# Looking up embeddings by one-hot matmuls and by gathers: nine features instead of seven in the first block, and one-hot work on both sides of the dot products

## Chip, core and metric
The kernel runs on one core of a Trainium2 chip. The metric is the device time of one execution in microseconds. TensorE (PE in the profile) multiplies, VectorE (DVE) and ScalarE (ACT) work element by element, GpSimd (POOL) issues the gathers here, and SyncE (SP) issues all other transfers. Each engine works through its own queue in order, and they meet at semaphores.

## What is computed
For each of 2048 samples, 27 rows of 128 numbers are looked up in 27 tables by the sample's ids. All 351 dot products between two different rows of a sample are taken, 16 dense numbers are appended, and three layers follow.

```
e = jnp.stack([tbl_0[ids[:, 0]], tbl_1[ids[:, 1]], ...], axis=1)
dot = jnp.einsum('bnd,bmd->bnm', inputs, inputs)
h = jnp.concatenate([z, dense_ctx], axis=1)
h = jnp.maximum(h @ W_top1 + b_top1, 0.0)
h = jnp.maximum(h @ W_top2 + b_top2, 0.0)
y = h @ W_top3
```

## The kernel before
The batch is cut into 8 blocks of 256 samples, a block into 2 tiles of 128. Two kinds of lookup exist.

**Gathered features.** 16 features (`GATHERED`) are fetched row by row: one indirect DMA on GpSimd's queue per feature and tile (line 353), into a ring of five buffers `rows` with four features each, a group. TensorE transposes a group into `tile_ps` (`tile_group`, line 605), ScalarE copies it into `samples` (`empty_group`, line 377). GpSimd may fill a ring buffer again when the group five before it has been transposed. Groups are counted through the kernel as n.

**One-hot features.** 11 features (`ONEHOT`) have tables of 1000 rows. Their tables are loaded once (line 238) through six staging buffers and split in a high half (`split_hi`, ScalarE, line 362) and a low half (`split_lo`, VectorE, line 501). For each block and feature SyncE loads the 256 ids, copied to all partitions (`idb`, line 229, a ring of three). VectorE compares them with row numbers (`masks`, line 494), and TensorE multiplies the masks with both halves (`onehot`, lines 593 and 595). A feature is four parts; a part is two masks and four matmuls. VectorE can be five parts ahead (`MASK_RING`), a block has 44 parts, counted from 0. Two features share a PSUM bank, a pair, which ScalarE copies out (`empty_onehot`, line 368).

**First block.** Its one-hots are made in a preamble, while tables still arrive. Only `NO_FIRST` = 7 features are looked up that way; the other four (`LATE`) are gathered for its two tiles, so these have five groups (20 gathers), all others four.

**Blocks.** Block b has 8 units. In each unit TensorE transposes the next tile's groups (`GROUPS_AT`), computes the dot products of 32 samples (`dot_unit`, line 621), and then does the unit's five or six parts for block b+1 (`unit_parts`, from `PARTS_UNTIL`). Layers of the block before follow: layer 3 in unit 0, the four steps of layer 1 in units 3 to 6, layer 2 in unit 7. `dot_unit` in units 0 and 4 waits until ScalarE has copied out all lookups of its samples. ScalarE copies dots out (`empty_dots`, line 396), and in block 0 splits w1 after unit 4's dots and w2 after unit 5's; VectorE makes their low halves after the masks of parts 28 and 33 (lines 509 and 516).

**SyncE's queue.** After a block SyncE issues, in this order: the ids of the third feature of the block after next (a load that waits until mask 43 is made), four stores of the dots to DRAM (line 269), one load of ids, the dense numbers, after the stores have landed the loads that bring the dots back with one product per partition (`load_z`, lines 278 and 280), and then the next ids. VectorE splits what came back in `z_hi` and `z_lo` (`split_z`, line 532) in unit 3, for layer 1. In the preamble the queue holds tables and ids by turns, then the weights (`load_weights`, lines 245 to 251), then the ids of block 1 from feature 3 on. The last block stores and reloads its dots in two halves.

## Time and profile before
| | |
|---|---|
| three runs | 379.4, 377.6, 384.47 us (median 379.4) |
| the profiled execution | 376.98 us, of which the span 375.2 us |
| mean granted clock of TensorE | 0.973 of full speed |
| TensorE busy | 331.5 us, 88% of the span |
| GpSimd busy | 252.3 us, 67%, in 264 gathers |
| VectorE busy | 250.1 us, 67% |
| ScalarE busy | 134.3 us, 36% |

Busy times of matmuls are modelled, and TensorE works on several at once. GpSimd's share leaves out the short pauses between gathers. An average over the span hides that the front (to about 100 us) and the tail (from about 342 us) have limits of their own, so the stretches are read one by one.

### The profile page before, as it was taken

The numbers are of one execution on the slowest core, as the hardware profiler recorded it, in microseconds if no ns is written. First come the engines' busy times: TensorE is split into PE (matmuls) and PEld (weight loads), VectorE is DVE, ScalarE is ACT, GpSimd is POOL, SyncE is SP. The second block draws the span as 40 slices with busy tenths as digits, with TensorE's granted clock in tenths as the row PEclk, the third lists the DMA queues.
The fourth block names the chain that finished last, engine by engine and source line by source line (L and its number), as shares of the span: only waits on it lengthen the run. The fifth ranks groups of instructions, "written<-read, shape, count | busy, mean of one in ns | idle before, by whom it ended". The sixth has DMA issues, their size and how long they took to land.

```text
span 375.2 us, 14179 instructions
## 1 busy us (share of the span) xinstructions
PE 331.5 (88%) x6216; PEld 302.7 (81%) x6216; DVE 250.1 (67%) x757; ACT 134.3 (36%) x235; POOL 252.3 (67%) x271
## 2 busy tenths in 40 slices
PE   0776679788799999999999999999899999996786
PEld 0665679678699988998999988998799988995775
DVE  3899577697477669765876769666776769622031
ACT  2353424532222533333333343333233343344122
POOL 5777777777777777777777777777777777760000
PEclk9999698999899999999999999999999999999699
DMA  7999954248644665348544754447634755354410
GB/s 171 239 214 231 225 142 100 81 94 190 115 91 96 141 146 113 84 90 193 127 80 101 162 131 105 93 107 178 112 87 94 163 125 113 79 120 90 79 41 1
DMA packets 59215, 46.39 MB, mean 124 GB/s; under 512 B 38499, under 2 KB 53186, under 8 KB 59153
## 3 DMA queue, kind: packets, MB, share of 16 engines
q1 hardware_dynamic: 50705, 28.16, 35.0%
q0 software_dynamic: 8448, 17.32, 19.6%
q8 instruction: 49, 0.80, 0.9%
q14 instruction: 13, 0.11, 0.1%
HBM read 38.37 MB, written 7.09 MB: 121 GB/s over the span
## 4 chain that ended last, share of the span: by engine, by line
PE 62%; DMA 12%; POOL 11%; DVE 8%; issue 6%; ACT 1%; POOLq 0%
PE onehot_ps L593 16%; PE onehot_ps L595 13%; POOL rows L353 11%; PE dots_ps L621 10%; DMA idb<-ids_onehot 8%; DVE mask L494 7%; PE tile_ps L605 6%; PE mlp_ps L627 5%; PE mlp_ps L629 5%; PE mlp_ps L628 5%; DMA rows<-tbl,idx 3%; PE mlp_ps L662 2%; DMA idx<-ids_gather 1%; DVE z_lo L532 0%; DVE z_hi L529 0%
## 5 line engine op out<-in xcount | busy, mean ns | idle before, releaser
L353 POOL DMA_INDIRECT rows<-tbl,idx x264 | 251.5, 953 | 82.5 <-issue 79.6
L494 DVE TENSOR_SCALAR mask<-idb,cmp 125x256 fp32r<-125x256 int32 x672 | 208.8, 381 | 54.1 <-PE onehot_ps L595 32.2
L593 PE MATMUL onehot_ps<-mask,tab_hi 125*128 125x256 f32 x672 | 175.9, 300 | 28.5 <-DVE mask L494 17.6
L595 PE MATMUL onehot_ps<-mask,tab_lo 125*128 125x256 f32 x672 | 166.3, 284 | 0.0
L593 PEld LDWEIGHTS onehot_ps<-mask,tab_hi 125*128 125x128 f32 x672 | 129.6, 193 | 35.7 <-DVE mask L494 17.1
L595 PEld LDWEIGHTS onehot_ps<-mask,tab_lo 125*128 125x128 f32 x672 | 130.3, 194 | 0.0
L621 PEld LDWEIGHTS dots_ps<-emb 128*27 128x27 f32 x4096 | 45.4, 106 | 19.6 <-issue 16.4
L377 ACT COPY emb<-tile_ps 128x512 f32<-128x512 f32 x66 | 44.1, 671 | 46.9 <-PE tile_ps L605 45.4
L621 PE MATMUL dots_ps<-emb 128*27 128x27 f32 x4096 | 54.8, 194 | 6.3 <-issue 5.6
L368 ACT COPY emb<-onehot_ps 128x512 f32<-128x512 f32 (+1 forms) x46 | 36.3, 789 | 57.3 <-PE onehot_ps L595 54.7
L605 PE MATMUL tile_ps<-ident,rows 128*128 128x128 f32 x264 | 40.9, 279 | 4.5 <-DMA rows<-tbl,idx 4.5
L539 DVE SCALAR_TENSOR_TENSOR h_lo<-mlp_ps,h_hi 128x512 fp32r<-128x512 f32 x16 | 11.1, 692 | 43.7 <-ACT h_hi L402 43.7
L605 PEld LDWEIGHTS tile_ps<-ident,rows 128*128 128x128 f32 x264 | 30.7, 143 | 7.8 <-issue 7.7
L396 ACT COPY dots<-dots_ps 128x216 f32<-128x216 f32 x64 | 21.7, 339 | 28.7 <-PE dots_ps L621 28.5
L627 PE MATMUL mlp_ps<-z_hi,w_hi 125*128 125x256 f32 (+1 forms) x96 | 28.2, 294 | 0.5 <-ACT h L421 0.5
L628 PE MATMUL mlp_ps<-z_hi,w_lo 125*128 125x256 f32 (+1 forms) x96 | 27.9, 290 | 0.0
L629 PE MATMUL mlp_ps<-z_lo,w_hi 125*128 125x256 f32 (+1 forms) x96 | 27.9, 290 | 0.0
L402 ACT ACTIVATE h_hi<-mlp_ps 128x512 fp32r<-128x512 f32 x16 | 9.6, 597 | 47.2 <-PE mlp_ps L629 47.2
L362 ACT CAST tab_hi<-emb 125x1024 fp32r<-125x1024 f32 x11 | 11.5, 1047 | 25.6 <-DMA emb<-tbl 25.6
L627 PEld LDWEIGHTS mlp_ps<-z_hi,w_hi 125*128 125x128 f32 (+1 forms) x96 | 19.1, 199 | 1.0 <-ACT h L421 1.0
L627 PE MATMUL mlp_ps<-h_hi,w_hi 128*128 128x256 f32 x64 | 18.2, 284 | 1.4 <-DVE h_lo L539 1.4
L628 PEld LDWEIGHTS mlp_ps<-z_hi,w_lo 125*128 125x128 f32 (+1 forms) x96 | 19.1, 199 | 0.0
(30 smaller groups left out, 153.0 us busy)
## 6 DMA issues: line engine op xcount, KB each, us to landing
idb<-ids_onehot SPq DMA_DIRECT2D x84, 128.0 KB
dots_dram<-dots SPq DMA_DIRECT2D x28, 216.0 KB
emb<-tbl SPq DMA_DIRECT2D x11, 448.0 KB
rows<-tbl,idx POOLq DMA_INDIRECT x264
zT<-dots_dram SPq DMA_DIRECT2D x14, 117.0 KB
dots_dram<-dots SPq DMA_DIRECT2D x8, 108.0 KB, 2.9
zT<-dots_dram SPq DMA_DIRECT2D x7, 104.0 KB
emb<-tbl SPq DMA_DIRECT2D x11, 52.0 KB
```

Of the source, the lines that this page charges most:

```text
L353: nc.gpsimd.indirect_dma_start(rows[:, n % RING, i, :], None, tables[feature][:, :], bass.IndirectOffsetOnAxis(idx[:, at:at + 1], 0)).then ...
L368: nc.scalar.copy(samples[b % 2][:, :, NG + a:NG + z], onehot_ps[:, pair(b, v) % 2, 0:(z - a) * BLK].rearrange("p (k b) -> p b k", k=z - a) ...
L377: nc.scalar.copy(samples[b % 2][:, q * P:(q + 1) * P, at:at + GROUP], tile_ps[:, n % 2, :].rearrange("p (k b) -> p b k", k=GROUP)).then_in ...
L396: nc.scalar.copy(dst[:, :, at:at + UNIT_Q], dots_ps[:, u % 2, 0:UNIT_Q * FEATURES].rearrange("p (c j) -> p j c", c=UNIT_Q)).then_inc(dots_ ...
L494: made = nc.vector.tensor_scalar(mask[0:VP, n % MASK_RING, c, :], idb[0:VP, k % IDB_RING, :], cmp[0:VP, at:at + 1], None, ALU.is_equal)
L593: nc.tensor.matmul(out, tab_hi[0:VP, f, at, :], mask[0:VP, k % MASK_RING, c, :], start=(at == 0), stop=False)
L595: done = nc.tensor.matmul(out, tab_lo[0:VP, f, at, :], mask[0:VP, k % MASK_RING, c, :], start=False, stop=(at == CHUNKS - 1))
L605: done = nc.tensor.transpose(tile_ps[:, n % 2, i * P:(i + 1) * P], rows[:, n % RING, i, :], ident[:, :])
L621: done = nc.tensor.matmul(dots_ps[PAD * s:PAD * s + FEATURES, u % 2, i * FEATURES:(i + 1) * FEATURES], sample, sample, start=True, stop=True)
L627: nc.tensor.matmul(out, w_hi, x_hi, start=first, stop=False)
L628: nc.tensor.matmul(out, w_lo, x_hi, start=False, stop=False)
L629: return nc.tensor.matmul(out, w_hi, x_lo, start=False, stop=last)
```

## The change
Nine features instead of seven are looked up by one-hot in the first block. The last group of its two tiles then has two gathers instead of four (`group_size`), 18 a tile; the index arrays and the counts of the `gathered` semaphores follow (`GROUP_AT`, `RING_USES`). Its transposes stand after other features (`FIRST_GROUPS_AT`). In each unit two parts now stand between the transposes and the dots, two between the dots and the layers, and the rest behind the layers, on TensorE and in ScalarE's copies. In the last block SyncE puts the dense numbers behind the first half's stores and loads that half back ahead of the second half's stores. VectorE's code is unchanged; its lookups follow `NO_FIRST`.

```
-NO_FIRST = 7
+NO_FIRST = 9
-NGR_FIRST = NGR + len(LATE) // GROUP
+NGR_FIRST = NGR + 1
+def group_size(g):
+    return GROUP if g < NGR else len(LATE)
+GROUP_LIST = [(t, g) for t in range(NT) for g in range(groups(t))]
+GROUP_AT = [sum(group_size(g) for _, g in GROUP_LIST[:n]) for n in range(len(GROUP_LIST) + 1)]
+BEFORE_DOTS, BEFORE_LAYERS = 2, 4
-FIRST_GROUPS_AT = {1: 0, 2: 1, 3: 2, 5: 3, 6: 4}
+FIRST_GROUPS_AT = {1: 0, 2: 1, 4: 2, 5: 3, 6: 4}
+def pair_ends(f, h):
+    return h == PARTS - 1 and (f % 2 == 1 or f == NO - 1)
...
# SyncE
+            for f in range(NO - NO_FIRST, IDB_RING):
+                load_idb(1, f)
             load_weights()
...
                 store_dots(LAST, q * P * half, dots[:, LAST % 2, q * half:(q + 1) * half], NQ // TILES,
                            last_out[q])
-            load_dense(LAST)
-            for q in range(TILES):
+                if q == 0:
+                    load_dense(LAST)
                 sp.wait_ge(last_out[q], 16 * QUAD)
...
# GpSimd
-                    for i in range(GROUP):
+                    for i in range(group_size(g)):
...
# ScalarE
+                    parts = unit_parts(u) if b < LAST else []
+                    for f, h in parts[:BEFORE_DOTS]:
+                        if pair_ends(f, h):
+                            empty_onehot(b + 1, f // 2)
                     empty_dots(b, u)
+                    for f, h in parts[BEFORE_DOTS:BEFORE_LAYERS]:
+                        if pair_ends(f, h):
+                            empty_onehot(b + 1, f // 2)
...
+                    for f, h in parts[BEFORE_LAYERS:]:
+                        if pair_ends(f, h):
+                            empty_onehot(b + 1, f // 2)
...
# TensorE
+                    for f, h in parts[:BEFORE_DOTS]:
+                        onehot(b + 1, f, h)
                     dot_unit(b, u)
-                    if b < LAST:
-                        for f, h in unit_parts(u):
-                            onehot(b + 1, f, h)
+                    for f, h in parts[BEFORE_DOTS:BEFORE_LAYERS]:
+                        onehot(b + 1, f, h)
                     if b > 1 and u == LAYER3_AT:
                         layer3(b - 2)
...
+                    for f, h in parts[BEFORE_LAYERS:]:
+                        onehot(b + 1, f, h)
```

TensorE, block 0, the start of unit 4. Before:

```order
L605 MATMUL tile_ps<-ident,rows 128x128 [waits gathered0,tile_ps_empty]
L605 MATMUL tile_ps<-ident,rows 128x128 x3
L621 MATMUL dots_ps<-emb 27x27 [waits onehot_ps_empty,tile_ps_empty,dots_ps_empty]
L621 MATMUL dots_ps<-emb 27x27 x31
L593 MATMUL onehot_ps<-mask,tab_hi 128x256 [waits mask_ready]
L595 MATMUL onehot_ps<-mask,tab_lo 128x256
```

The same place in the changed kernel:

```order
L631 MATMUL tile_ps<-ident,rows 128x128 [waits gathered0,tile_ps_empty]
L631 MATMUL tile_ps<-ident,rows 128x128 x3
L619 MATMUL onehot_ps<-mask,tab_hi 128x256 [waits mask_ready,onehot_ps_empty]
L621 MATMUL onehot_ps<-mask,tab_lo 128x256
L619 MATMUL onehot_ps<-mask,tab_hi 128x256
L621 MATMUL onehot_ps<-mask,tab_lo 128x256
L619 MATMUL onehot_ps<-mask,tab_hi 128x256 [waits mask_ready]
L621 MATMUL onehot_ps<-mask,tab_lo 128x256
L619 MATMUL onehot_ps<-mask,tab_hi 128x256
L621 MATMUL onehot_ps<-mask,tab_lo 128x256
L647 MATMUL dots_ps<-emb 27x27 [waits onehot_ps_empty,tile_ps_empty,dots_ps_empty]
L647 MATMUL dots_ps<-emb 27x27 x31
```

Eight one-hot matmuls, two parts, have moved ahead of the unit's 32 dot products (line 621 before is line 647 now).

SyncE, the end of the preamble's queue, from the last id load ahead of the weights on. Before:

```order
L229 DMA idb<-ids_onehot 128x256 [waits mask_ready]
L238 DMA emb<-tbl 112x1024 [waits lo_ready]
L238 DMA emb<-tbl 13x1024
L245 DMA dots<-w 125x512 x2
L245 DMA dots<-w 117x512
L247 DMA dots<-b 1x512
```

In the changed kernel:

```order
L246 DMA idb<-ids_onehot 128x256 [waits mask_ready]
L255 DMA emb<-tbl 112x1024 [waits lo_ready]
L255 DMA emb<-tbl 13x1024
L246 DMA idb<-ids_onehot 128x256 [waits mask_ready] x2
L262 DMA dots<-w 125x512 x2
L262 DMA dots<-w 117x512
L264 DMA dots<-b 1x512
```

Two id loads, each waiting for masks, now stand between the last table and the weights.

ScalarE, block 0, units 6 and 7 (lines 377, 396 and 368 copy a transposed group, dots, and a one-hot pair). Before:

```order
L377 COPY emb<-tile_ps 128x128x4 [waits tile_ps_full]
L396 COPY dots<-dots_ps 128x27x8 [waits dots_ps_full]
L377 COPY emb<-tile_ps 128x128x4 [waits tile_ps_full]
L396 COPY dots<-dots_ps 128x27x8 [waits dots_ps_full]
L368 COPY emb<-onehot_ps 128x256x2 [waits mask_used]
L368 COPY emb<-onehot_ps 128x256 [waits mask_used]
```

In the changed kernel:

```order
L400 COPY emb<-tile_ps 128x128x4 [waits tile_ps_full]
L419 COPY dots<-dots_ps 128x27x8 [waits dots_ps_full]
L400 COPY emb<-tile_ps 128x128x4 [waits tile_ps_full]
L390 COPY emb<-onehot_ps 128x256x2 [waits mask_used]
L419 COPY dots<-dots_ps 128x27x8 [waits dots_ps_full]
L390 COPY emb<-onehot_ps 128x256 [waits mask_used]
```

The copy of the pair that ends with part 39 now stands ahead of the copy of unit 7's dots.

## Rows read from the trace of the kernel before

**Rows 1.** Page, costly groups: line, engine, operation, count | busy us, mean ns | idle before

```profile
L353 POOL DMA_INDIRECT rows<-tbl,idx x264 | 251.5, 953 | 82.5 <-issue 79.6
```

**Rows 2.** Timeline of GpSimd: start us, us, engine, line, operation [idle before, releaser]

```profile
334.62 0.95 POOL L353 DMA_INDIRECT rows<-tbl,idx  x1 [0.31 <-issue]
```

**Rows 3.** Time windows: window, busy us per engine, granted clock, DMA share, GB/s

```profile
core 0: us, PE busy (x) PEld busy (x) DVE busy (x) ACT busy (x) POOL busy (x), PEclk, DMA share, GB/s
40.00:88.50 48.50, 41.41 (x817) 37.94 (x818) 36.10 (x109) 18.39 (x34) 36.64 (x39) 0.91 0.58 134
...
56.00:58.00 2.00, 2.00 (x11) 2.00 (x11) 2.00 (x8) 0.71 (x1) 1.64 (x2) 0.50 0.39 87
...
131.00:173.00 42.00, 41.50 (x788) 38.19 (x787) 30.17 (x99) 15.09 (x27) 31.86 (x34) 1.00 0.55 122
...
135.11:137.92 2.81, 2.81 (x24) 2.81 (x25) 2.13 (x8) 1.16 (x2) 2.20 (x3) 1.00 0.60 178
```

**Rows 4.** Timeline of TensorE, transposes at unit 7, unit 4 and unit 7

```profile
121.68 0.60 PE L605 MATMUL tile_ps<-ident,rows 128*128 128x128 f32 x4
...
148.45 0.60 PE L605 MATMUL tile_ps<-ident,rows 128*128 128x128 f32 x4
...
163.05 0.60 PE L605 MATMUL tile_ps<-ident,rows 128*128 128x128 f32 x4
```

**Rows 5.** Timeline of TensorE, block 0

```profile
40.56 1.09 PE L605 MATMUL tile_ps<-ident,rows 128*128 128x128 f32 x4 [3.43 <-DMA rows<-tbl,idx]
...
54.12 0.38 PE L593 MATMUL onehot_ps<-mask,tab_hi 125*128 125x256 f32 x1 [2.04 <-DVE mask L494]
...
63.31 0.60 PE L605 MATMUL tile_ps<-ident,rows 128*128 128x128 f32 x4
...
69.67 0.39 PE L593 MATMUL onehot_ps<-mask,tab_hi 125*128 125x256 f32 x1 [1.45 <-DVE mask L494]
```

**Rows 6.** Timeline of VectorE, preamble to block 1

```profile
30.30 1.26 DVE L501 TENSOR_TENSOR tab_lo<-emb,tab_hi 125x1024 fp32r<-125x1024 f32 x1
...
34.04 1.27 DVE L501 TENSOR_TENSOR tab_lo<-emb,tab_hi 125x1024 fp32r<-125x1024 f32 x1
35.23 3.16 DVE L494 TENSOR_SCALAR mask<-idb,cmp 125x256 fp32r<-125x256 int32 x10
...
53.45 6.63 DVE L494 TENSOR_SCALAR mask<-idb,cmp 125x256 fp32r<-125x256 int32 x22 [2.69 <-DMA idb<-ids_onehot]
...
67.13 1.90 DVE L509 TENSOR_TENSOR w_lo<-dots,w_hi 125x512 fp32r<-125x512 f32 x3 [2.32 <-ACT w_hi L426]
...
75.54 9.31 DVE L494 TENSOR_SCALAR mask<-idb,cmp 125x256 fp32r<-125x256 int32 x30
...
98.62 2.48 DVE L494 TENSOR_SCALAR mask<-idb,cmp 125x256 fp32r<-125x256 int32 x8 [4.75 <-DMA idb<-ids_onehot]
```

**Rows 7.** Timeline of SyncE's queue, preamble, and the stores after blocks 0 and 1

```profile
37.24 1.08 SPq L245 DMA_DIRECT2D dots<-w  x3
...
43.31 18.84 SPq L229 DMA_DIRECT2D idb<-ids_onehot  x6
...
82.03 4.05 SPq L269 DMA_DIRECT2D dots_dram<-dots  x4
...
125.31 4.22 SPq L269 DMA_DIRECT2D dots_dram<-dots  x4
```

**Rows 8.** Timeline of ScalarE, the copy of the pair that ends with part 31

```profile
71.70 0.79 ACT L368 COPY emb<-onehot_ps 128x512 f32<-128x512 f32 x1 [2.85 <-PE onehot_ps L595]
```

**Rows 9.** Timeline of VectorE, block 2

```profile
140.60 2.51 DVE L494 TENSOR_SCALAR mask<-idb,cmp 125x256 fp32r<-125x256 int32 x8 [1.76 <-DMA idb<-ids_onehot]
...
146.98 0.42 DVE L532 TENSOR_TENSOR z_lo<-zT,z_hi 118x256 fp32r<-118x256 f32 x1
```

**Rows 10.** Timeline of TensorE, layer 1 of the last block

```profile
363.21 0.39 PE L627 MATMUL mlp_ps<-z_hi,w_hi 125*128 125x256 f32 x1 [0.45 <-ACT h L421]
```

More of the change, by code:

```diff
@@ L84, in group_slot @@
     return GROUP * g if g < NGR else NG + NO_FIRST
+def group_size(g):
+    return GROUP if g < NGR else len(LATE)
+GROUP_LIST = [(t, g) for t in range(NT) for g in range(groups(t))]
+GROUP_AT = [sum(group_size(g) for _, g in GROUP_LIST[:n]) for n in range(len(GROUP_LIST) + 1)]
+RING_USES = [sum(group_size(GROUP_LIST[k][1]) for k in range(n % RING, n + 1, RING)) for n in range(len(GROUP_LIST))]
 UNIT_Q = 8
@@ L142, in build @@
         rows = sb("rows", [P, RING, GROUP, D], f32)
-        idx = sb("idx", [P, group(NT, 0) * GROUP], i32)
+        idx = sb("idx", [P, GROUP_AT[-1]], i32)
         idb = sb("idb", [P, IDB_RING, BLK], i32)
@@ L350, in _ @@
                         pool.wait_ge(tile_ps_full, n - RING + 1)
-                    for i in range(GROUP):
-                        feature, at = SLOTS[group_slot(g) + i], GROUP * n + i
+                    for i in range(group_size(g)):
+                        feature, at = SLOTS[group_slot(g) + i], GROUP_AT[n] + i
                         nc.gpsimd.indirect_dma_start(
@@ L365, in empty_onehot @@
             def empty_onehot(b, v):
+                if b == 1 and v == 0:
+                    act.wait_ge(lo_ready, NO)
                 a, z = 2 * v, min(2 * v + 2, looked_up(b))
@@ L376, in empty_group @@
                 act.wait_ge(tile_ps_full, n + 1)
-                nc.scalar.copy(samples[b % 2][:, q * P:(q + 1) * P, at:at + GROUP],
-                               tile_ps[:, n % 2, :].rearrange("p (k b) -> p b k", k=GROUP)
+                k = group_size(g)
+                nc.scalar.copy(samples[b % 2][:, q * P:(q + 1) * P, at:at + k],
+                               tile_ps[:, n % 2, 0:k * P].rearrange("p (k b) -> p b k", k=k)
                                ).then_inc(tile_ps_empty, 1)
@@ L602, in tile_group @@
                     pe.wait_ge(tile_ps_empty, n - 1)
-                pe.wait_ge(gathered[n % RING], 16 * GROUP * (n // RING + 1))
-                for i in range(GROUP):
+                pe.wait_ge(gathered[n % RING], 16 * RING_USES[n])
+                for i in range(group_size(g)):
                     done = nc.tensor.transpose(tile_ps[:, n % 2, i * P:(i + 1) * P], rows[:, n % RING, i, :],
@@ L677, in _ @@
                     t = TILES * b + u // UNITS_TILE + 1
+                    parts = unit_parts(u) if b < LAST else []
                     for g in GROUPS_AT[u % UNITS_TILE]:
@@ L680, in _ @@
                             tile_group(t, g)
+                    for f, h in parts[:BEFORE_DOTS]:
+                        onehot(b + 1, f, h)
                     dot_unit(b, u)
-                    if b < LAST:
-                        for f, h in unit_parts(u):
-                            onehot(b + 1, f, h)
+                    for f, h in parts[BEFORE_DOTS:BEFORE_LAYERS]:
+                        onehot(b + 1, f, h)
                     if b > 1 and u == LAYER3_AT:
@@ L734 @@
         "ids_gather": _np.stack([ids[t * P:(t + 1) * P, SLOTS[group_slot(g) + i]] for t in range(NT)
-                                 for g in range(groups(t)) for i in range(GROUP)], axis=1),
+                                 for g in range(groups(t)) for i in range(group_size(g))], axis=1),
         "ids_onehot": ids[:, ONEHOT].T,
```

4 lines of the change are left out of this document (removed).

## Prediction

> **What bounds the kernel now.** I read the page's table of costly groups first, then the time windows, then the timelines of each engine in the first two blocks and in one later block.
>
> GpSimd issues 264 gathers of 0.95 us with 0.30 us between them [rows 1]. The last starts at 334.62 us [rows 2]: 264 x 1.256 = 331.6 us, so it runs almost from start to end of that stretch without a wait. It looks like the pace setter and is not: from the second block on it is several groups ahead. TensorE in block 2 is busy 41.50 of 42 us [rows 3]; a later block is bound by TensorE. From unit 7 to unit 7 a block takes 163.05 - 121.68 = 41.37 us [rows 4].
>
> Block 0 is different. TensorE is busy only 41.41 of 48.5 us, part of it at half clock: the granted clock in 56 to 58 us is 0.50 [rows 3], 1.2 of 2.4 GHz, after 2.04 us of idling [rows 5]. Its waits are for gathered rows (3.43 us at 40.56) and for masks (2.04 at 54.12, 1.45 at 69.67) [rows 5]. VectorE in turn waits there for a feature's ids (2.69) and for ScalarE's half of the w1 split (2.32) [rows 6]. So the front of the kernel hangs on VectorE, its inputs and SyncE's queue, the rest on TensorE.
>
> **Prices.** A part (4 matmuls of 256 columns) costs TensorE 2.81 / 6 = 0.47 us [rows 3]. VectorE makes 30 masks in 9.31 us [rows 6], 0.62 us a part. From the tile transposes at 63.31 to part 29 at 69.67 [rows 5] lie two transposes-plus-dots, five parts and the wait: (6.36 - 1.45 - 2.35) / 2 = 1.28 us for one group's transposes with one unit of dots, of which I give 0.75 to the dots.
>
> **Four gathers fewer.** They take 4 x 1.256 = 5.0 us off GpSimd. Between 0 and -5.0 us; I take 0, because the gathers for block 2 on are finished before they are wanted. The 3.43 us wait at 40.56 goes too, but the next item covers it.
>
> **Two more features in the preamble.** 16 masks, 2 table splits (moved forward), 32 matmuls. The splits of consecutive features start 34.04 - 30.30 = 3.74 us apart [rows 6], and that is VectorE's pace per feature, TensorE's matmuls hiding behind it. Before, the last mask of the preamble is done at about 35.9 (the first pair of the ten from 35.23 [rows 6]); now 35.9 + 7.5 = 43.4. The 12 parts of block 1 that follow, with the one split left, need 12 x 0.62 + 1.2 = 8.6 us: VectorE wants the ids of feature 3 at 52.0.
>
> **SyncE's queue.** It now issues two more id loads before the weights, and the last of these waits for all 36 preamble parts (43.4). The weights therefore start at 43.9 instead of 37.24, and since they take 43.31 - 37.24 = 6.1 us to issue [rows 7], the ids of feature 3 are issued at 50.0 instead of 43.31. Before, they landed at 53.45 [rows 6], 10.1 us after issue, queued behind weights and a table. The price now is not in the trace. The table is older by then, the weights are not. Floor: landed before they are wanted, 52.0. Ceiling: again 10.1 us, 60.1. I take 54.7, nearer the floor: the same bytes as before plus two id loads (0.25 MB at the 134 GB/s of this stretch [rows 3] is 1.9 us at most, and I take 1.3) after the old 53.4. TensorE resumes at 55.4, 1.3 us later than at 54.12.
> The Trainium skill (DMA: Bandwidth & Descriptors, Latency and other measured facts) speaks of about 2 us of fixed cost per DMA. By it alone the load would be in at about 52 and VectorE would not wait; the old load's 10.1 us speaks against using it with a full queue.
>
> **Interleaving in block 0.** From part 12 to unit 4's transposes it took 63.31 - 54.12 = 9.19 us [rows 5]; one unit of dots more and two transposes less give 9.85: unit 4 starts at 65.25 (+1.9). The w1 split in ScalarE's queue sits behind the dots of unit 4, VectorE's half behind it [rows 6], and masks from part 29 on behind that. Two parts now stand ahead of these dots: 0.94 us more. Part 29 starts at 65.25 + 6.36 + 0.94 = 72.55 (+2.9). The w2 split comes after ScalarE's copy of the pair that ends with part 31, which was at 71.70 [rows 8]; a unit of dots now stands between parts 30 and 31: 0.7 us more. Part 34's mask starts at 72.55 + (75.54 - 69.67) + 0.7 = 79.1 against 75.54, part 43's is made 6.2 us later, at 85.3, and SyncE, which waits for it with an id load ahead of the stores, starts storing at 85.6 against 82.03 [rows 7]: **+3.6 us**. Bounds: 0 if the ids are never late, +6 if the 3.1 us idling that this puts before parts 29 and 34 drops the clock as 2.04 us did.
>
> **Block 1** follows the stores: from there to the mask of part 16, which had waited 4.75 us for its ids, 98.62 - 82.03 = 16.6 us [rows 6, 7]. Same chain, +3.6 us stays.
>
> **Blocks 2 to 6.** Take L, the end of layer 1's fourth step, as zero (121.68 [rows 4]). Then the stores start at 3.6 (125.31 [rows 7]), released by mask 43 and not by the dots; mask 16 starts at 18.9 and z_lo's third part is done at 25.7 [rows 9]; unit 4 starts at 26.8 (148.45) and the next L comes 14.6 later [rows 4]. The new order moves the dots of unit 7 to L + 2.9, still done with their copy when mask 43 is. So the DMA chain stays. On TensorE one part less lies before layer 1's first step (part 38 went behind L, parts 22 and 23 behind the step): it waits for z_lo until 25.7, ends at 26.1, parts 22 and 23 put unit 4 at 27.0 (+0.2), and the rest is 14.1 (-0.5). 41.1 instead of 41.37. Bounds -0.6 and +1.2 a block; I take -0.2, five times: **-1.1**. The ends of the chain: -0.5 in block 1 (part 38), +0.4 before block 7 (part 43 behind layer 2).
>
> **The last block.** The dense load goes ahead of the second half's stores, and z of the first half is loaded ahead of them. TensorE's start on the last block's layer 1 at 363.21 waits for ScalarE (0.45 us), not for z [rows 10]. 0.
>
> **Sum:** 3.6 - 0.5 - 1.1 + 0.4 = +2.4 us on the profiled execution's 376.98 us (span 375.2), 379.4. That execution is 2.4 us under the 379.4 us median of the runs, and the fastest run is 377.6; I state the forecast between these two scales, **380.0 us**.
>
> **Rivals.**
> - *The gathers are the pace after all.* Then 5.0 us come through and with them the 3.43 us wait: 376.98 - 8.4 = 368.5. For it: 331.6 us without a gap [rows 1, 2]. Against: TensorE at 41.50 of 42 [rows 3]. 0.10.
> - *The ids of feature 3 land in time* (below 52.0). Then VectorE never stops, the clock stays up, and unit 4 starts at 61.5 to 62.7: 2.6 to 3.8 us off the sum, 375.6 to 376.8, a small gain. 0.15.
> - *The loop gets longer (the other side).* The dots of unit 7 now come 1.4 us later after L, and ScalarE copies a one-hot pair (0.79 us [rows 8]) ahead of theirs. If that copy ends more than about 0.3 us after mask 43, the stores move, and with them everything to z_lo: 0.7 to 1.2 us in each of six blocks, 4 to 7 us: 383.6 to 386.6. The idling before parts 29 and 34 adds up to 2.4 at half clock: up to 389. 0.20.
> - *Nothing adds:* within 376.8 to 383, the forecast. 0.50. The remaining 0.05 lies above 389.
>
> **How the numbers follow.** The range takes in the second rival, the forecast and most of the third: 373 to 388. A change of 2% is 7.6 us, about what a measurement of this kernel can tell from none. Faster by over 2%: the first rival and a little, 0.12. Slower: most of the third and the rest, 0.20. Within: 0.68.
>
> **What would show it.** In the changed profile: preamble one-hots end near 44 with no wait for gathered rows after them; the first mask wait in block 0 near part 12 at 54 to 55; waits of about 3 us before parts 29 and 34; first stores at 85 to 86; block period 41.1 with a wait for z_lo before layer 1; GpSimd waiting for transposes for the first time. The forecast is wrong if the first stores come before 82, or if the period is below 40.5 or above 42.

## The result: slower, with the loss in the front

| | before | after |
|---|---|---|
| four runs each, same chip | 377.6 to 384.47 us, median 380.23 | 385.76 to 387.23 us, median 386.95 |
| ratio (95% interval) | | 1.024 (1.020 to 1.028) |
| span of the profiled execution | 375.2 us | 385.2 us |
| mean granted clock of TensorE | 0.973 | 0.969 |

The changed kernel is 6.7 us slower by the medians, 2.4%. The time lies inside the forecast range (373 to 388), 7 us above the forecast itself. I called a change within 2% likeliest; the kernel is slower beyond its interval, by about 2% or a little more. In a second measurement the changed kernel had 387.09 us against 379.32 (1.016, 0.996 to 1.037). Here and below a median takes all executions, a ratio leaves out those over 1.5% above the fastest of their kernel, so the two need not agree. The profiled execution of before is 3.3 us under the median of its runs, so the spans differ by more than the medians, 10.0 us; the steps below are followed on that scale.

The page of the changed kernel, TensorE's two rows of slices, the group that answers to [rows 1], and TensorE's one-hots:

```profile
PE   0867859779869999999999999999999998997777
PEclk9999997969969999999999999999999999999899
...
L372 POOL DMA_INDIRECT rows<-tbl,idx x260 | 249.5, 960 | 90.0 <-issue 74.8
L619 PE MATMUL onehot_ps<-mask,tab_hi 125*128 125x256 f32 x688 | 190.7, 309 | 33.6 <-DVE mask L520 23.0
```

Four gathers fewer bring nothing here: GpSimd now idles instead, as its pauses for transposes show (13.0 us in 14 of them). The granted clock falls in slices 7, 9 and 12, which begin at 58, 77 and 106 us. TensorE waited 23.0 us for masks in all.

**The front.** TensorE, at the places of [rows 5] and at the start of block 1:

```profile
58.16 0.58 PE L619 MATMUL onehot_ps<-mask,tab_hi 125*128 125x256 f32 x1 [5.09 <-DVE mask L520]
...
68.31 0.60 PE L631 MATMUL tile_ps<-ident,rows 128*128 128x128 f32 x4
...
75.42 0.38 PE L619 MATMUL onehot_ps<-mask,tab_hi 125*128 125x256 f32 x1 [2.77 <-DVE mask L520]
...
83.36 0.39 PE L619 MATMUL onehot_ps<-mask,tab_hi 125*128 125x256 f32 x1 [2.48 <-DVE mask L520]
...
91.92 0.60 PE L631 MATMUL tile_ps<-ident,rows 128*128 128x128 f32 x4
...
109.08 0.55 PE L619 MATMUL onehot_ps<-mask,tab_hi 125*128 125x256 f32 x1 [4.82 <-DVE mask L520]
```

Part 12 comes 4.0 us later than before, unit 4's transposes 5.0, part 29 5.75. Part 34 comes 7.15 later (before it stood at 76.21 after a wait of 1.96), block 1 8.8 (before at 83.11). The three waits ahead of parts 12, 29 and 34 are 5.09, 2.77 and 2.48 us, where 2.04, 1.45 and 1.96 had stood.

VectorE, at the places of [rows 6]:

```profile
46.34 5.01 DVE L520 TENSOR_SCALAR mask<-idb,cmp 125x256 fp32r<-125x256 int32 x16
57.46 2.63 DVE L520 TENSOR_SCALAR mask<-idb,cmp 125x256 fp32r<-125x256 int32 x8 [6.10 <-DMA idb<-ids_onehot]
...
72.88 1.89 DVE L535 TENSOR_TENSOR w_lo<-dots,w_hi 125x512 fp32r<-125x512 f32 x3 [3.44 <-ACT w_hi L449]
...
80.84 1.10 DVE L542 TENSOR_TENSOR w_lo<-zT,w_hi 128x256 fp32r<-128x256 f32 x3 [3.12 <-ACT w_hi L455]
...
82.68 1.55 DVE L520 TENSOR_SCALAR mask<-idb,cmp 125x256 fp32r<-125x256 int32 x5
```

It stands idle 6.10 us for the ids of feature 3, then 3.44 and 3.12 us for ScalarE's halves of the splits. SyncE's queue, the answer to [rows 7]:

```profile
43.20 2.12 SPq L262 DMA_DIRECT2D dots<-w  x3
...
49.48 2.23 SPq L246 DMA_DIRECT2D idb<-ids_onehot  x3
...
90.89 4.27 SPq L286 DMA_DIRECT2D dots_dram<-dots  x4
```

The weights are issued from 43.20 instead of 37.24, the ids of feature 3 at 49.48 instead of 43.31, and they are in at 57.46. The first stores start at 90.89, 8.9 us later.

What releases these stores is new. The mask for part 43 is made at 89.23 (end of the six masks from 87.33), but the stores start 0.02 us after ScalarE's copy of unit 7's dots, which is done at 90.87:

```profile
87.33 1.90 DVE L520 TENSOR_SCALAR mask<-idb,cmp 125x256 fp32r<-125x256 int32 x6 [0.35 <-PE onehot_ps L621]
...
90.53 0.34 ACT L419 COPY dots<-dots_ps 128x216 f32<-128x216 f32 x1 [0.46 <-PE dots_ps L647]
```

Before, that copy was done at 81.13, ahead of mask 43 (about 81.7, an estimate from the pace of the 30 masks in [rows 6]), and the stores followed the mask.

**Windows** of the changed kernel, the answer to [rows 3] (busy us per engine, granted clock, DMA share, GB/s):

```profile
42.00:44.00 2.00, 1.16 (x10) 1.16 (x11) 2.00 (x8) 1.43 (x2) 1.49 (x2) 1.00 0.50 86
44.00:46.00 2.00, 2.00 (x76) 1.83 (x75) 2.00 (x6) 1.08 (x3) 1.39 (x3) 1.00 0.33 48
46.00:48.00 2.00, 1.82 (x13) 1.48 (x13) 2.00 (x7) 0.08 (x1) 1.70 (x2) 1.00 0.55 194
...
58.00:60.00 2.00, 1.84 (x8) 1.78 (x8) 2.00 (x7) 0.00 (x0) 1.41 (x2) 0.50 0.26 66
...
78.00:80.00 2.00, 2.00 (x11) 2.00 (x11) 0.00 (x0) 1.18 (x4) 1.70 (x2) 0.50 0.59 109
...
84.00:86.00 2.00, 2.00 (x68) 1.77 (x69) 2.00 (x8) 0.00 (x0) 1.39 (x3) 0.50 0.51 78
```

And two of these windows in the kernel before:

```profile
42.00:44.00 2.00, 2.00 (x55) 1.94 (x45) 0.26 (x1) 0.00 (x0) 1.70 (x2) 0.50 1.09 212
44.00:46.00 2.00, 2.00 (x15) 2.00 (x15) 1.83 (x7) 1.35 (x2) 1.39 (x3) 0.78 1.13 246
```

From 42 to 46 us the transfers move 86 and 48 GB/s where they had moved 212 and 246: the weights, the next large transfers in the queue, stand behind an id load that waits for masks. They are issued from 43.20 on, but it is 46 us before the rate is up again (194). After each of the three waits in block 0 there are windows at half clock (0.50, 1.2 GHz).

**Blocks 2 to 6.** TensorE's transposes at unit 7 of block 1 and of block 6, and layer 1's wait for z_lo in block 2:

```profile
131.91 0.60 PE L631 MATMUL tile_ps<-ident,rows 128*128 128x128 f32 x4
...
157.23 0.39 PE L653 MATMUL mlp_ps<-z_hi,w_hi 118*128 118x256 f32 x1 [0.51 <-DVE z_lo L558]
...
339.83 0.60 PE L631 MATMUL tile_ps<-ident,rows 128*128 128x128 f32 x4
```

Before, the last of these stood here:

```profile
330.20 0.60 PE L605 MATMUL tile_ps<-ident,rows 128*128 128x128 f32 x4
```

The period, the average length of these blocks, is (339.83 - 131.91) / 5 = 41.58 us; before, (330.20 - 121.68) / 5 = 41.70 us over the same five blocks, with 121.68 from [rows 4]. These blocks are as long as they were: the loss is there by 132 us. The average before holds one long block (246.04 to 288.92, 42.88 us); its other four took 41.28 to 41.59 us, the five of the changed kernel 41.38 to 41.91. A last 0.6 us is added behind block 7's first transposes (346.32, where 336.91 stood, +9.4).

### The profile page after: what moved, and what is told of

It is laid out like the page before. It is cut to its first block, busy times and chain, and to the rows that moved or that the text cites. A ratio compares the mean times of both kernels' runs of the same rounds, so it can differ in the third digit from the quotient of the medians.

```text
span 385.2 us, 14253 instructions
## 1 busy us (share of the span) xinstructions
PE 336.6 (87%) x6244; PEld 309.6 (80%) x6244; DVE 256.1 (66%) x773; ACT 134.5 (35%) x236; POOL 250.3 (65%) x267
## 4 chain that ended last, share of the span: by engine, by line
PE 50%; DVE 17%; DMA 16%; SPq 11%; issue 3%; ACT 3%; DVEq 0%
PE onehot_ps L619 14%; PE onehot_ps L621 12%; DVE mask L520 11%; PE dots_ps L647 8%; DMA dots_dram<-dots 7%; DMA idb<-ids_onehot 6%; PE tile_ps L631 4%; SPq L295 4%; SPq L286 4%; PE mlp_ps L653 4%; PE mlp_ps L655 3%; PE mlp_ps L654 3%; DVE tab_lo L527 3%; DMA emb<-tbl 2%; DVE z_lo L558 1%
## 5 line engine op out<-in xcount | busy, mean ns | idle before, releaser
L520 DVE TENSOR_SCALAR mask<-idb,cmp 125x256 fp32r<-125x256 int32 x688 | 214.7, 381 | 50.6 <-DMA idb<-ids_onehot 25.5
L619 PE MATMUL onehot_ps<-mask,tab_hi 125*128 125x256 f32 x688 | 190.7, 309 | 33.6 <-DVE mask L520 23.0
L621 PE MATMUL onehot_ps<-mask,tab_lo 125*128 125x256 f32 x688 | 176.1, 287 | 0.0
L619 PEld LDWEIGHTS onehot_ps<-mask,tab_hi 125*128 125x128 f32 x688 | 134.6, 196 | 42.6 <-DVE mask L520 23.0
L621 PEld LDWEIGHTS onehot_ps<-mask,tab_lo 125*128 125x128 f32 x688 | 135.3, 197 | 0.2 <-issue 0.2
L400 ACT COPY emb<-tile_ps 128x512 f32<-128x512 f32 (+1 forms) x66 | 44.7, 678 | 50.0 <-PE tile_ps L631 49.9
L419 ACT COPY dots<-dots_ps 128x216 f32<-128x216 f32 x64 | 21.7, 339 | 81.3 <-PE dots_ps L647 73.9
L390 ACT COPY emb<-onehot_ps 128x512 f32<-128x512 f32 (+1 forms) x47 | 37.2, 791 | 35.1 <-PE onehot_ps L621 35.1
L631 PE MATMUL tile_ps<-ident,rows 128*128 128x128 f32 x260 | 39.7, 275 | 0.0
L655 PEld LDWEIGHTS mlp_ps<-z_lo,w_hi 125*128 125x128 f32 (+1 forms) x96 | 18.8, 196 | 0.0
```

Of the source, the lines that this page charges most:

```text
L390: nc.scalar.copy(samples[b % 2][:, :, NG + a:NG + z], onehot_ps[:, pair(b, v) % 2, 0:(z - a) * BLK].rearrange("p (k b) -> p b k", k=z - a) ...
L400: nc.scalar.copy(samples[b % 2][:, q * P:(q + 1) * P, at:at + k], tile_ps[:, n % 2, 0:k * P].rearrange("p (k b) -> p b k", k=k)).then_inc( ...
L419: nc.scalar.copy(dst[:, :, at:at + UNIT_Q], dots_ps[:, u % 2, 0:UNIT_Q * FEATURES].rearrange("p (c j) -> p j c", c=UNIT_Q)).then_inc(dots_ ...
L520: made = nc.vector.tensor_scalar(mask[0:VP, n % MASK_RING, c, :], idb[0:VP, k % IDB_RING, :], cmp[0:VP, at:at + 1], None, ALU.is_equal)
L619: nc.tensor.matmul(out, tab_hi[0:VP, f, at, :], mask[0:VP, k % MASK_RING, c, :], start=(at == 0), stop=False)
L621: done = nc.tensor.matmul(out, tab_lo[0:VP, f, at, :], mask[0:VP, k % MASK_RING, c, :], start=False, stop=(at == CHUNKS - 1))
```

## Experiments

Each ratio is to the kernel before, measured alongside on the same chip, with its 95% interval. Times in the text are of the profiled execution, from the start of its span. "Unit 4" is block 0's.

### One part of the change alone

Nine features, with the old order and the old last block:

```
-BEFORE_DOTS, BEFORE_LAYERS = 2, 4
+BEFORE_DOTS, BEFORE_LAYERS = 0, 8
 # SyncE, last block: load_dense(LAST) and all loads of z behind both halves' stores again
```

> Nine features in the first block with everything else as before (parts all behind the unit's dots, last block's loads as before). Theory 1 (the front: two more features push the weights behind two id loads that wait for masks, the ids of feature 3 land at about 57 and TensorE takes up part 12 at about 58 instead of 54.12): 382 to 385 us, about 5 to 7 us over before, of which 4 us are there at part 12 and the rest comes from clock and block 1. Waits before parts 29 and 34 as before, 1.5 and 2 us. Rival 2 (the new order is what costs, the nine features are nearly free): at most 380 us.

Measured: median 381.76 us, ratio 1.005 (1.001 to 1.009), span 377.2. It came below the 382 to 385 us that I expected.

```profile
68.27 0.60 PE L631 MATMUL tile_ps<-ident,rows 128*128 128x128 f32 x4
...
74.65 0.39 PE L619 MATMUL onehot_ps<-mask,tab_hi 125*128 125x256 f32 x1 [1.45 <-DVE mask L520]
```

Unit 4 is as late as in the changed kernel (68.27 and 68.31): the delay up to there comes from the two features. The waits ahead of parts 29 and 34 are the old ones (1.45, and 1.02). The stores start at 87.04, +5.0 us. Blocks 2 to 6, at 41.41 us each, give back 1.5 us of it, and the span ends at +2.0.

The new order with seven features, and the old last block:

```
-NO_FIRST = 9
+NO_FIRST = 7
-FIRST_GROUPS_AT = {1: 0, 2: 1, 4: 2, 5: 3, 6: 4}
+FIRST_GROUPS_AT = {1: 0, 2: 1, 3: 2, 5: 3, 6: 4}
```

> The new order alone: seven features, parts on both sides of the dots, last block's loads as before. Theory 1: the ids of feature 3 land at 53.4 as before; only the waits before parts 29 and 34 grow (from 1.45 and 1.96 to about 2.8 and 2.5 us, with half clock behind them): 379 to 381.5 us, 2 to 4 us over before; block period 41.3 to 41.6 us. Rival 2: 384 us and more.

Measured: median 382.24 us, ratio 1.008 (1.003 to 1.012), span 380.9.

```profile
76.66 0.39 PE L619 MATMUL onehot_ps<-mask,tab_hi 125*128 125x256 f32 x1 [3.23 <-DVE mask L520]
...
121.92 0.60 PE L631 MATMUL tile_ps<-ident,rows 128*128 128x128 f32 x4
...
190.74 0.39 PE L653 MATMUL mlp_ps<-z_hi,w_hi 118*128 118x256 f32 x1 [0.98 <-DVE z_lo L558]
...
335.07 0.60 PE L631 MATMUL tile_ps<-ident,rows 128*128 128x128 f32 x4
```

The order alone lengthens the waits ahead of parts 29 (2.12 us at 69.29) and 34 (3.23), though the clock stays up here and the stores start only 1.2 us late (83.24). What it loses it loses later: (335.07 - 121.92) / 5 = 42.63 us a block, with a wait of about 1 us for z_lo in each. The changed kernel has the same code in these blocks and takes 41.58. I had expected 41.3 to 41.6, and 379 to 381.5 us in all; that difference gets two runs below.

With the clock up, this run also tells what the order costs at the end of block 0. The mask of part 34 starts at 75.94 and the stores at 83.24, again 0.02 us after the dots' copy:

```profile
82.88 0.34 ACT L419 COPY dots<-dots_ps 128x216 f32<-128x216 f32 x1 [0.65 <-PE dots_ps L647]
```

That is 7.30 us, where it takes 6.49 us in the kernel before and 6.48 with nine features in the old order.

The changed kernel with the last block as before:

```
-                if q == 0:
-                    load_dense(LAST)
+            load_dense(LAST)
+            for q in range(TILES):
                 sp.wait_ge(last_out[q], 16 * QUAD)
```

> The changed kernel with only the last block's stores and loads put back to the order of before. Theory: the three short waits of the last layer 1 for z_lo (0.99, 0.28 and 0.31 us) go and ScalarE's 0.45 us comes back: 0.3 to 0.8 us less than the changed kernel. Rival: the tail's 0.7 us is scatter of the dots' stores, no difference beyond 0.3 us.

Measured: median 384.73 us, ratio 1.015 (1.008 to 1.022), span 382.5. From block 7's first transposes (344.48) to the end it takes 38.0 us; the changed kernel 385.2 - 346.32 = 38.9. TensorE, last layer 1, changed kernel:

```profile
372.57 0.35 PE L653 MATMUL mlp_ps<-z_hi,w_hi 125*128 125x256 f32 x1 [0.99 <-DVE z_lo L558]
```

Two more waits for z_lo follow, of 0.28 and 0.31 us. With the old last block the same place has the 0.45 us wait for ScalarE of [rows 10] again, and none for z_lo. So with the first half loaded back ahead, layer 1 waits for what comes last. The price is not shown: that stretch takes 38.0 to 39.7 us in the three profiles with the new order and the old last block, and 38.4 to 40.7 us in the eight with the new one, and the measured times do not separate it either. On this chip the parts add up: by the medians the two features cost 2.2 us, the order 2.7, both together (this run) 5.2.

### Mending one suspected cost

The weights behind block 1's first ids:

```
-            load_weights()
             for b in range(BLOCKS):
...
                 if b < LAST:
                     load_idb(b + 1, IDB_RING)
+                if b == 0:
+                    load_w1()
...
                     for f in range(IDB_RING + 2, NO):
                         load_idb(b + 1, f)
+                        # b == 0: w2 and w3 follow the ids of the sixth and the seventh feature
```

> The changed kernel with SyncE's weights issued behind the ids of block 1: w1 and b1 behind feature 3's ids, w2 behind feature 5's, w3 and b2 behind feature 6's. Theory 1: VectorE's 6.10 us wait for ids shrinks to 1 us or less, part 12 starts at 53 to 54 instead of 58.16, no half clock there, unit 4 of block 0 at 62 to 63 instead of 68.31; 380.5 to 383 us. Rival 3 (the DMA engines are short there in any order, the wait only moves to a later id load): part 12 early, but another id wait of 3 us or more behind it, 385 us or more.

Measured: median 384.43 us, ratio 1.012 (1.004 to 1.021), span 379.1.

```profile
58.01 0.36 PE L627 MATMUL onehot_ps<-mask,tab_hi 125*128 125x256 f32 x1 [1.59 <-DVE mask L528]
...
63.44 0.60 PE L639 MATMUL tile_ps<-ident,rows 128*128 128x128 f32 x4
```

The wait of 5.09 us at part 12 is gone. The one of 1.59 us is a new one, four parts later: VectorE waits 2.80 us (to 57.18) for the ids of feature 4, which now stand behind w1. So the late load was in part only moved, as the rival had it, but by less than the 3 us named there. Unit 4 starts at 63.44, where it had started before the change, 4.9 us earlier than in the changed kernel, and the stores start at 86.07 (90.89): the weights ahead of the ids cost 4.9 us there. The profile, of the fastest of the four executions (380.86), shows it more plainly than the times, whose median came above what I expected (380.5 to 383).

Then the changed kernel once more, on the chip of the next three:

> The changed kernel once more, as the yardstick of the three below on one chip: 1.5 to 2.5% over before, id wait of 5 to 6 us in block 0, waits before parts 29 and 34 of 2.5 to 3 us.

Measured: median 387.09 us (382.37 to 390.74) against 379.32 (ratio above). The profiled execution (388.53) waits at the same places, ahead of parts 12, 29 and 34: 5.34, 2.93 and 3.37 us. Its period is 42.04 us, where the first profile had 41.58.

ScalarE's halves of the w1 and w2 splits one unit earlier:

```
-                    if b == 0 and u == 4:
+                    if b == 0 and u == 3:
                         split_w1_hi()
-                    if b == 0 and u == 5:
+                    if b == 0 and u == 4:
                         split_w2_hi()
```

> The changed kernel with ScalarE's halves of the w1 and w2 splits one unit earlier in its queue, behind units 3 and 4 of block 0 instead of 4 and 5. Theory (VectorE waits for ScalarE, who waits for a unit's dots that now come two parts later): VectorE's waits of 3.44 and 3.12 us go, TensorE's 2.77 and 2.48 us before parts 29 and 34 shrink below 0.5 us each and the half clock there with them, block 1 starts 4 to 6 us earlier, the whole is 4 to 6 us shorter than the changed kernel. Rival (VectorE is simply behind with its masks): the waits move to parts 30 to 38, less than 2 us shorter.

Measured: median 379.9 us, ratio 1.008 (1.003 to 1.014), span 379.3. The median is 7.2 us under the changed kernel's on the same chip; by the ratios (1.008 against 1.016, the latter with a wide interval) it is some 3 us, and by the spans of the two profiles (379.3 and 385.2) 5.9.

```profile
84.48 0.60 PE L631 MATMUL tile_ps<-ident,rows 128*128 128x128 f32 x4
```

One wait of 0.58 us is left of the two, the clock stays up from 64 to 100 us, and block 1 starts at 84.48 instead of 91.92, 7.4 us earlier. The part-12 wait is untouched (4.82). So the splits that stand behind the dots in ScalarE's queue are the larger of the two costs.

Both together:

> The changed kernel with both of the two mends of its front: the weights behind block 1's first ids, and ScalarE's halves of the w1 and w2 splits one unit earlier. My theory: what the change loses in the front is the late weights queue (4.9 us up to unit 4 of block 0, in the run with the weights moved) and the two mask waits behind the splits with their half clock (some 6 us, in the run with the splits moved), and the two are at different places, so they add up: block 1 starts at 79.5 to 81 us instead of 91.9, and the time falls to 374 to 377 us, below the kernel before. Rival: the second is only hidden idling of the same DMA or mask chain, so that the two together give what one gave: 379 to 381 us. In both the block period stays at 41.6 us.

Measured: median 376.84 us, ratio 0.996 (0.991 to 1.001), span 374.9.

```profile
58.42 0.35 PE L627 MATMUL onehot_ps<-mask,tab_hi 125*128 125x256 f32 x1 [2.02 <-DVE mask L528]
...
81.37 0.60 PE L639 MATMUL tile_ps<-ident,rows 128*128 128x128 f32 x4
```

Block 1 starts at 81.37, 10.5 us earlier than in the changed kernel: more than either alone (4.8 and 7.4), less than their sum. The wait at 58.42, part 16's, is followed by half clock here, and unit 4 starts at 65.45 instead of 63.44. With both mended the front's loss is gone, and the kernel is level with the one before. The period was 41.83 us, where I had expected 41.6.

### What sets the length of blocks 2 to 6

By the prediction's step on these blocks it is the chain stores, loads of z, ids, masks, z_lo. If so, an id load that stands behind the loads of z, and with them behind the wait for the stores, is what to move. In the kernel before:

```
                 if b > 0:
                     load_dense(b - 1)
+                if b < LAST:
+                    load_idb(b + 1, IDB_RING + 1)
+                if b > 0:
                     sp.wait_ge(dots_out[(b - 1) % 2], 16 * QUAD * ((b - 1) // 2 + 1))
                     load_z(b - 1, 0, slice(0, BLK), NQ, z_in)
-                if b < LAST:
-                    load_idb(b + 1, IDB_RING + 1)
```

> The kernel before, with one load of ids (feature 4 of the next block) moved ahead of the wait for the stores and the loads of z in SyncE's queue. Theory (in the old order the chain stores, z loads, ids, masks, z_lo is just short of being the limit, except in blocks 1 and 5): VectorE's wait for ids before part 16 goes (4.75 us in block 1), TensorE's 2.64 us there too; the period of blocks 2 to 6 falls from 41.7 to 40.8 to 41.2 us; 4 to 7 us under before. Rival (TensorE's work is the period): only block 1 gains, 2 to 3 us.

Measured: median 373.56 us, ratio 0.989 (0.977 to 1.002), span 371.7. Unit 7 of block 1, of block 6, and a transpose of the last tile:

```profile
121.72 0.60 PE L606 MATMUL tile_ps<-ident,rows 128*128 128x128 f32 x4
...
323.76 0.60 PE L606 MATMUL tile_ps<-ident,rows 128*128 128x128 f32 x4
...
338.84 0.41 PE L606 MATMUL tile_ps<-ident,rows 128*128 128x128 f32 x2 [3.31 <-DMA rows<-tbl,idx]
```

The period is 40.41 us, 1.3 less, and of VectorE's waits for ids in blocks 2 to 6 one of 0.15 us is left. TensorE has the same work in these blocks, so its work was not what set their length before. The interval of the ratio still reaches 1. Now GpSimd is late at the end: TensorE waits 3.31 us for rows that did not hold it up before.

The same move in the changed kernel:

> The changed kernel with the same move of one id load. Theory (in the new order that chain is the period): the waits for z_lo before layer 1 (0.5 to 0.9 us a block) go, the period falls from 41.6 to 40.8 to 41.1 us, TensorE's 4.82 us wait in block 1 shrinks below 1.5 us: 6 to 9 us under the changed kernel. Rival (the z loads are what is late, not the masks queued ahead of the z splits): the waits for z_lo stay, at most 4 us, all from block 1.

Measured: median 377.52 us, ratio 0.998 (0.993 to 1.002), span 375.5. The median is 9.6 us under the changed kernel's on the same chip, the span 9.7 us under the 385.2 of its first profile. The period is (330.36 - 127.14) / 5 = 40.64 us, the waits for z_lo are gone there, and block 1's wait at part 16 falls from 4.82 to 0.94. The three waits of block 0 stay (4.75, 2.46, 2.94).

### All of it: what order and features are worth then

The changed kernel with all three mends:

> The same with the id load of a block's fifth feature ahead of the loads that bring the dots back. It took the block period from 41.6 to 40.7 us in the changed kernel. If that holds here too, 4.6 us come off: 369.5 to 372.5 us. Rival: GpSimd now limits (its 260 gathers of 1.256 us cannot have the last one started before 329.6 us), shown by waits for gathered rows in the last two blocks: 373 us or more.

Measured: median 368.63 us, ratio 0.975 (0.970 to 0.981), span 367.3, period 40.84. That is a little under what I expected. There is no wait for rows in the last two blocks, but GpSimd never pauses for more than 0.31 us, and its last gather starts at 330.84.

The same with the old order in every unit:

> The same again, but with a unit's parts all behind its dots, as in the kernel before, in every unit (nine features in the first block, the new last block). If the interleaved order costs something by itself wherever VectorE's masks are short, this one is faster by up to 2 us: 368.5 to 371 us, with a period of 40.4. Rival: with the waits gone the order is worth something, and this one is slower than the interleaved kernel of this call by over 1 us.

Measured: median 367.63 us, ratio 0.975 (0.969 to 0.981), span 366.2, period 40.51. The two cannot be told apart by time (367.16 to 369.51 and 367.17 to 369.9). That does not show that the order is worth nothing. With the old order TensorE comes to block 7 3.8 us earlier (324.29 against 328.08) and then waits 1.87 and 2.18 us for rows, so that its last transposes start at 333.65, against this in the new order:

```profile
334.32 0.66 PE L640 MATMUL tile_ps<-ident,rows 128*128 128x128 f32 x4
```

In both the last gather starts at 330.8 us. The gathers hide what the old order gains; what it would be worth without them is not measured.

The kernel before with the same three mends:

> The kernel before (seven features, its own order, 264 gathers) with the same three mends. It tells what the two features more are worth once nothing else is in the way. GpSimd's last gather cannot start before 334.6 us here, against 329.6 with 260 gathers. If GpSimd limits by now, it waits for rows in block 0 and in the last two blocks and takes 2 to 4 us more than the nine-feature kernel in the same order: 372 to 374 us. Rival: the preamble, 7.5 us shorter on VectorE, gives more than the gathers cost: 367 to 370 us, below the nine-feature kernel.

Measured: median 372.58 us, ratio 0.988 (0.982 to 0.993), span 370.6, period 40.67. Two of its rows, TensorE's last wait for gathered rows and GpSimd's last gather (in block 0 it also waits 2.97 and 2.57 us for rows):

```profile
338.74 1.09 PE L614 MATMUL tile_ps<-ident,rows 128*128 128x128 f32 x4 [3.26 <-DMA rows<-tbl,idx]
...
335.56 0.94 POOL L362 DMA_INDIRECT rows<-tbl,idx  x1 [0.30 <-issue]
```

With nine features, old order:

```profile
333.65 1.09 PE L640 MATMUL tile_ps<-ident,rows 128*128 128x128 f32 x4 [2.18 <-DMA rows<-tbl,idx]
...
330.85 1.09 POOL L381 DMA_INDIRECT rows<-tbl,idx  x1 [0.30 <-issue]
```

Now the last gather is what the end waits for. It starts 4.7 us earlier with nine features, and TensorE's last transposes 5.1 us earlier. That is close to the 5.0 us between the medians, and to the 4 x 1.256 us of the prediction's step on the gathers. The two kernels differ in the last block too, which is 0.7 us longer in the nine-feature one from there to the end. What was worth nothing in the change is worth some 5 us here: the kernel had to be limited by GpSimd first.

### Why 42.63 and 41.58 us with the same code

GpSimd paused for about 2 us beside stores and loads of z in the changed kernel, and never with seven features. To force the pause with seven, four ring buffers instead of five:

```
-RING = 5
+RING = 4
```

> Seven features in the new order, with a ring of four instead of five buffers for gathered rows. With five, its blocks 2 to 6 took 42.64 us each though the changed kernel, with the same code there, took 41.58. My theory: GpSimd's gathers share the DMA engines with the loads that bring the dots back. In the changed kernel GpSimd is ahead and pauses for about 2 us, for a ring buffer, just while stores and loads are under way; with seven features it never pauses, and the chain from the first store to z_lo's third part takes 22.4 to 23.0 us instead of 21.6. With four buffers it must pause there too: the chain falls to 21.6 to 21.8 and the period to 41.5 to 41.9. The total may rise, since block 0 has less in store. Rival: the 1 us comes from where the features' masks lie or from the place of the instructions, and period and chain stay at 42.4 or more.

Measured: median 383.75 us, ratio 1.010 (1.005 to 1.015), span 380.7, period 42.06. From the stores to z_lo's third part it took 22.7, 22.2, 21.9, 21.9 and 22.1 us in blocks 2 to 6, with pauses of about 2 us in all in the last two alone. The period lies between what the two theories gave. The chain is shorter than with five buffers (22.4 to 23.0), but no shorter where the pauses are: block 4, without one, has the same 21.9 as block 5 with one.

The changed kernel with the last two features of the first tiles gathered twice (the index arrays and the semaphore counts follow):

```
-                    for i in range(group_size(g)):
-                        feature, at = SLOTS[group_slot(g) + i], GROUP_AT[n] + i
+                    for i in range(GROUP):
+                        feature, at = SLOTS[group_slot(g) + i % group_size(g)], GROUP_AT[n] + i
```

> The changed kernel, but each of the first block's two tiles gathers its last two features twice, so that GpSimd issues 264 gathers as before (the second copies are not used). It prices the four gathers fewer by themselves. By my prediction they are worth 0. By the theory of the pauses GpSimd gets ahead 5 us later, so that in some blocks it does not pause beside the loads: up to 1 us a block, 387 to 391 us, with a chain of 22.4 us or more in each block where no pause of GpSimd falls in the first 9 us after the stores start. Rival: nothing hangs on them, 385.5 to 387.5 us, with the period at 41.6.

Measured: median 387.12 us, ratio 1.014 (1.002 to 1.025), span 385.8, period 41.83. The changed kernel had 386.95 and 387.09 in its two measurements. These times could not tell 4 us from nothing, but the profile agrees with 0, as predicted: TensorE waits for rows only once, 0.84 us in the preamble, and GpSimd still pauses, 6.9 us in all. Block 3 of this run, stores and z_lo's third part, with no pause of GpSimd in between:

```profile
176.08 3.98 SPq L286 DMA_DIRECT2D dots_dram<-dots  x4
...
197.47 0.42 DVE L558 TENSOR_TENSOR z_lo<-zT,z_hi 118x256 fp32r<-118x256 f32 x1
```

That is 21.4 us. Block 5, with a pause:

```profile
259.12 2.50 SPq L286 DMA_DIRECT2D dots_dram<-dots  x3
...
263.11 0.95 POOL L372 DMA_INDIRECT rows<-tbl,idx  x1 [1.02 <-PE tile_ps L631]
...
281.71 0.43 DVE L558 TENSOR_TENSOR z_lo<-zT,z_hi 118x256 fp32r<-118x256 f32 x1
```

That is 22.6 us, longer with the pause than without. So the theory of the pauses falls. With the id load in its old place the chain takes 20.8 to 23.1 us in blocks 2 to 6 of these profiles, and what makes it 22.4 or more in all five blocks of the one kernel stays open. Each kernel has one profile here, the changed one two, whose periods (41.58 and 42.04) lie 0.46 us apart. Whether 42.63 belongs to the kernel or to that one execution is not shown.

## Why the prediction came out as it did

**Right.** *Four gathers fewer, 0*: the last run agrees, and GpSimd waits for transposes, as said. *The preamble*: the last masks ahead of the ids end at 51.4 (forecast: ids wanted at 52.0), weights issued from 43.2 (43.9), ids at 49.5 (50.0). *The places of the new waits*: parts 12, 29 and 34, with the splits behind the dots as cause of the last two. *Layer 1 bound by the DMA chain*: moving one id load shortened the block by 0.9 to 1.3 us.

**Right by luck.** *Blocks 2 to 6*: -0.12 us a block on average against -0.2, with the wait for z_lo. But 41.1 us was forecast and 41.58 came, and the difference is below zero only because before has its long block of 42.88 us, which the forecast did not know; against the other four it is +0.17. (The -0.2 was rough too: 41.1 against 41.37 is -0.27, and five times -0.2 is -1.0, not -1.1.)

**Wrong, and by how much** (together 7.6 us of span: 10.0 against a sum of 2.4):

- *The landing of the ids in "SyncE's queue".* I took 54.7 and wrote that the same bytes would follow in a full queue. They landed at 57.46, 8.0 us after issue. The step that failed is "the same bytes as before plus two id loads": it has the bytes flow on as before, but the weights were issued 6.0 us later, because they waited for the 36th part's masks, and from 42 to 46 us the DMA engines moved 86 and 48 GB/s instead of 212 and 246. The ids landed 4.0 us later than before and not 1.3. Part 12 was +4.0 us instead of +1.3, and part 29 +5.75 instead of +2.9. That the weights are the cause is shown by the run that moved them. My 54.7 lay about as far below the landing as the ceiling of 60.1 above it. The Trainium skill (DMA: Bandwidth & Descriptors, Latency and other measured facts) has about 2 us of fixed cost per DMA; the 8.0 us here, behind the weights, neither bear that out nor speak against it.
- *From part 12 to unit 4.* It took 10.15 us. The 9.85 of the forecast does not come out of its own terms either: 9.19 + 0.75 less two transposes is about 9.7. This is inside the +5.75 at part 29.
- *The half clock behind the new waits.* I had it as a bound and a rival, "up to 2.4", and not in the sum. From part 29 to the mask of part 34 it took 7.26 us instead of 6.55; ScalarE's copy ahead of the w2 split waits for one-hots in windows of 0.70 and 0.50 clock there. With seven features in the new order, where the clock stayed at 1.00, the same stretch took 6.65.
- *What releases the first stores.* I had mask 43, 6.5 us after the mask of part 34. It took 8.21, and the release was the dots' copy, 1.6 us behind mask 43. At full clock this is 7.30 us with seven features and the new order, and 6.5 in the old order with seven or nine. So about 0.8 us is the new order, and the 0.9 left goes with the half clock (0.50 and 0.74 in 84 to 88 us). With the 0.7 us of the stretch ahead of it: stores at +8.9, where the forecast had +3.6.
- *Block 1, "same chain".* The chain from stores to part 16's mask took 17.4 instead of 16.6 us. From there to unit 7's transposes it took 23.6 instead of 23.1, where 0.5 less was forecast for part 38. Together 1.9 us.
- *The last block, 0.* It was +0.6 us, with waits for z_lo; the profiles scatter by more than that there.
- Against the forecast, blocks 2 to 6 give +0.5 and the step to block 7 gives -0.6. (All these are rounded.)

Two readings of the kernel before were wrong without moving the sum. "A later block is bound by TensorE" came from 41.50 busy of 42 us; moving one id load took 1.3 us off the same work. And GpSimd was not "several groups ahead" from the second block on: TensorE waited 0.61 and 0.49 us for rows in block 1 (at 88.47 and 93.25), and 3.31 us at the end once the blocks were shorter. The signs of a wrong forecast that I named (first stores before 82, a period below 40.5 or above 42) did not show either, since for the stores I had named only the early side.

The rival on the other side, "the loop gets longer", gave the right range of times (up to 389). Its mechanism, the dots' copy behind mask 43, came once, in block 0, for 0.8 us at full clock. In blocks 1 to 5 that copy is done 0.4 to 0.5 us before the stores start, and the loop did not get longer by it; the half clock that the rival names did come. The rival on the gathers was wrong for this change and right for the kernel one step further.

## What to carry to other kernels

When work is added in front of a queued load that waits for that work, look at what the DMA engines do meanwhile. Here the rate fell for 4 us, large loads came 6 us later, and the small load behind them was late by 4 us. (No run filled the stretch by putting the weights ahead of the two waiting id loads; the runs put them behind.) A copy that another engine waits for should not stand behind a long step in an in-order queue; moving two of them by one unit let block 1 start 7.4 us earlier. And a saving on an engine that runs without a gap counts only after the limit of the others has gone below it: the four gathers were worth nothing that could be seen in this change and some 5 us after three moves of loads and copies.

## What the chip showed that I had not expected

- **A wait of 2 to 3 us may or may not cost the clock.** Before, the wait of 2.04 us at part 12 was followed by half clock in 56 to 58 us [rows 3, 5]. With seven features in the new order a wait of 3.23 us (at 76.66) was followed by a window at 1.00, in the changed kernel one of 2.48 us (at 83.36) by half clock (0.50 in 84 to 86). With both front mends, 2.02 us at 58.42 was followed by 0.50 two us later, and 1.59 us with the weights' mend alone by none. The length of the wait did not decide it alone; what did stays open.

A window behind the wait of 3.23 us (seven features, new order):

```profile
77.00:79.00 2.00, 2.00 (x74) 1.78 (x73) 2.00 (x8) 0.00 (x0) 1.69 (x2) 1.00 0.33 84
```

and of 2.02 us (both front mends):

```profile
60.50:62.50 2.00, 2.00 (x12) 1.78 (x11) 1.99 (x7) 0.99 (x2) 1.55 (x2) 0.50 0.73 124
```

- **The same chain of transfers varies.** From the stores' start to z_lo's third part it took 20.8 to 23.1 us, in blocks with the same code. The block's length moves with it: in the kernel before, the one block with 23.1 us took 42.88 us, the other four, with 21.6 to 21.7, took 41.28 to 41.59.
